# A norm between two layers, and the order in which weight tiles are streamed behind it

## The reference

```python
def attn(x):            # 16 query heads in 4 groups, head size 128, causal
    q, kg, vg = x @ Wq + bq, x @ Wk + bk, x @ Wv + bv
    return softmax(mask(q @ k.T / sqrt(128))) @ v
def ternary_quant(w):   # one scale for the whole matrix
    s = mean(abs(w))
    return clip(round(w / s), -1, 1) * s
def ffn(x):             # hidden size 5461
    h1, h3 = x @ ternary_quant(w1).T, x @ ternary_quant(w3).T
    return (silu(h1) * h3) @ ternary_quant(w2).T
x = layernorm(x + attn(x))
x = layernorm(x + ffn(x))
```

## Time and profile before

| what | before |
|---|---|
| median of 3 runs (lowest, highest) | 1499.0 us (1335.76, 1522.67) |
| the profiled execution's own time | 1341.49 us |
| its span (slowest core; all cores) | 1339.9 us (1333.4 to 1339.9) |
| PE busy, share of the span | 1272.4 us, 95% |
| DVE, ACT, POOL busy | 832.1, 458.5, 80.9 us |
| DMA, mean over the span | 321.52 MB, 240 GB/s |

### The profile page before, as it was taken

One profiled execution on the slowest core, in us unless ns is written; L12 is line 12 of the kernel. 1 busy time (PEld: TensorE's weight loads), 2 busy tenths in 40 slices (PEclk: granted clock), 3 DMA queues, 4 the chain that ended last, 5 costly groups with the idle time before them and its releaser, 6 DMA issues.

```text
span 1339.9 us, 18596 instructions; the slowest of 8 cores (1333.4 to 1339.9 us)
## 1 busy us (share of the span) xinstructions
PE 1272.4 (95%) x6824; PEld 616.3 (46%) x6824; DVE 832.1 (62%) x1200; ACT 458.5 (34%) x562; POOL 80.9 (6%) x150
## 2 busy tenths in 40 slices
PE   4999999999979889899999999999999999999996
PEld 1344556666655334344444444444444444444443
DVE  0222467777784436577766676766794388585864
ACT  0031478877887553633123232230100400000005
POOL 4000000000010000101000000000000010000000
PEclk9999999999999999899999999999999999999999
DMA  9999999999789998899867777675452964435326
GB/s 151 174 246 280 314 276 266 281 277 269 242 265 338 322 336 266 280 330 342 282 244 251 274 256 286 244 248 215 146 201 69 308 244 149 157 135 172 126 87 253
DMA packets 47761, 321.52 MB, mean 240 GB/s; under 512 B 5296, under 2 KB 5552, under 8 KB 11824
## 3 DMA queue, kind: packets, MB, share of 16 engines
q1 hardware_dynamic: 26640, 188.12, 42.2%
q0 software_dynamic: 21024, 132.13, 33.5%
HBM read 324.42 MB, written 16.78 MB: 255 GB/s over the span
## 4 chain that ended last, share of the span: by engine, by line
PE 84%; DMA 9%; DVE 3%; issue 2%; ACT 1%; POOL 1%; DVEq 0%; ACTq 0%; SPq 0%; POOLq 0%
PE ps L905 40%; PE ps L1102 22%; PE ps L413 7%; DMA ST<-w_sb 5%; PE ps L473 4%; PE ps L514 4%; DMA X<-xT 4%; PE ps L369 3%; PE ps L353 3%; PE ps L683 1%; DVE QNX L588 0%; DVE XR L536 0%; ACT PT L487 0%; DVE ACC L319 0%; ACT XB L666 0%
## 5 line engine op out<-in xcount | busy, mean ns | idle before, releaser
L905 PE MATMUL ps<-XT,QNL 128*128 128x512 bf16 x2048 | 442.4, 379 | 0.0
L905 PEld LDWEIGHTS ps<-XT,QNL 128*128 128x128 bf16 x2048 | 200.4, 98 | 241.4
L1102 PE MATMUL ps<-W2Q,G 128*128 128x512 bf16 x1376 | 297.5, 379 | 0.9 <-DVE G L928 0.6
L1102 PEld LDWEIGHTS ps<-W2Q,G 128*128 128x128 bf16 x1376 | 134.5, 98 | 163.7 <-issue 1.8
L487 ACT ACTIVATE PT<-ps 128x768 bf16<-128x768 f32 (+3 forms) x176 | 148.6, 867 | 79.1 <-PE ps L473 75.0
L588 DVE SCALAR_TENSOR_TENSOR QNL<-ST,SM,QNL 128x1024 bf16<-128x1024 f32 x128 | 164.4, 1285 | 13.7 <-DVE QNL L586 0.5
L918 ACT ACTIVATE SIL<-ps,SM 128x512 f32<-128x512 f32 x52 | 35.7, 687 | 297.0 <-PE ps L905 284.3
L316 ACT ACTIVATE ST<-ST 128x1024 f32<-128x1024 f32 (+1 forms) x79 | 108.1, 1369 | 69.7 <-DMA ST<-w_sb 69.5
L413 PE MATMUL ps<-X,WQ 128*128 128x512 bf16 x512 | 130.2, 379 | 0.8 <-DVE RCA L533 0.8
L588 DVE SCALAR_TENSOR_TENSOR W2Q<-W2F,SM,W2Q 128x1024 bf16<-128x1024 f32 x88 | 110.9, 1260 | 9.2
L905 PE MATMUL ps<-XT,QNE 128*128 128x512 bf16 x416 | 95.9, 391 | 13.0 <-DVE QNE L588 10.5
(11 more groups left out here) (73 smaller groups left out, 878.6 us busy)
## 6 DMA issues: line engine op xcount, KB each, us to landing
ST<-w_sb SPq DMA_DIRECT2D x167, 1024.0 KB, 11.0
W2F<-w_sb POOLq DMA_DIRECT2D x80, 1024.0 KB, 7.4
X<-xT POOLq DMA_DIRECT2D x16, 512.0 KB, 51.3
WQ<-wq_sb POOLq DMA_DIRECT2D x16, 512.0 KB, 12.1
XR<-xq POOLq DMA_DIRECT2D x8, 1024.0 KB, 35.8
x1spill<-XR POOLq DMA_DIRECT2D x8, 1024.0 KB, 24.8
out<-X SPq DMA_DIRECT2D x7, 1024.0 KB, 4.1
W2F<-w_sb POOLq DMA_DIRECT2D x8, 768.0 KB, 6.3
```

The source lines that it names most:

```text
L905: t = put("pe", lambda e, ec=ec: e.matmul(bank(b), qn(k)[:, ec * 128:(ec + 1) * 128], XT[:, ec * 1024 + hf * 512:ec * 1024 + (hf + 1) * 51 ...
L1102: return put("pe", lambda e: e.matmul(bank(t), G[hc][:, t * 128:(t + 1) * 128], W2Q[j % 5][:, hl * 512:(hl + 1) * 512], start=(hc == 0), s ...
```

## The change

Five edits:

- `LATE` is written anew. The number of "a" tiles behind each "w" tile, for k = 3 to 16, goes from 4 2 2 2 2 2 2 2 1 1 0 0 0 5 to 3 1 2 1 2 1 2 1 2 1 2 1 1 5; both add up to 25.
- At the last head, slots 4 and 5 are no longer spilled by `o_evac` in the norm. Their two DMAs are issued by POOL after the last kept tile has landed, and w2's loads wait for them.
- The sums of the 5 kept tiles are taken on VectorE (`tensor_reduce`, which writes no tile), instead of on ScalarE with a copy written to `W2F`.
- `o_evac(15, 5)` goes behind `ln_scale(0)` and the first two `ln_bf` of VectorE.
- The half of an absolute sum that VectorE still has to do when attention ends (`dve_bg`) goes behind `ln_stats((4, 5, 6, 7))`.

```diff
--- before.py
+++ after.py
@@ -259,7 +259,7 @@
         NWT = len(WT)
         PRE = 8
         EARLY = [3, 2, 6]
-        LATE = [4, 2, 2, 2, 2, 2, 2, 2, 1, 1, 0, 0, 0, 5]
+        LATE = [3, 1, 2, 1, 2, 1, 2, 1, 2, 1, 2, 1, 1, 5]
         spq = [("a", j) for j in range(PRE + 42)]
         ja = PRE + 42
         for k in range(NF):
@@ -306,13 +306,7 @@
                 a = col(ACC, which * 96 + ab_col[which])
                 ab_col[which] += 1
                 b = ST[s][:, k * n:(k + 1) * n]
-                if eng == "act" and j >= NAB - KEEP:
-
-                    junk = W2F[j % 3]
-                    toks.append(put("act", lambda e, a=a, b=b, junk=junk: e.activation(
-                        junk[:], b, AF.Abs, accum_out=a), [t_ab[j]] + w2_free[j % 3]))
-                    w2_free[j % 3] = [toks[-1]]
-                elif eng == "act":
+                if eng == "act":
                     toks.append(put("act", lambda e, a=a, b=b: e.activation(b, b, AF.Abs, accum_out=a),
                                     [t_ab[j]]))
                 else:
@@ -523,6 +517,7 @@
                 q_free[h + 3] = [t]
 
         t_res, t_spl = [None] * 8, [None] * 8
+        SPL_LATE = (4, 5)
         t_bn = {}
 
         def o_evac(h, ob):
@@ -540,7 +535,7 @@
             t_orel[ob] = [t]
             bfree[ob] = [t]
             if h == HH - 1:
-                for s in ss:
+                for s in [s for s in ss if s not in SPL_LATE]:
                     t_spl[s] = dma("pool", d_sp[s], XR[s][:], "spl%d" % s, [t])
 
         def bnst(s, c):
@@ -857,11 +852,6 @@
                 elif u == 10:
                     ln_stats((3,))
             if gi == NST - 1:
-                while dve_bg:
-                    try:
-                        next(dve_bg[0])
-                    except StopIteration:
-                        dve_bg.pop(0)
                 for b in range(4):
                     bfree[b] = [t_ex[NST - 2 + b // 2]]
 
@@ -869,14 +859,13 @@
 
         put("act", lambda e: e.activation(col(SM, 120), col(CFT, C_EPS), AF.Sqrt), [t_cf])
         n_att = ab_next[0]
-        if not general:
-            o_evac(HH - 1, 5)
         t = ln_scale(0)
         t_nm[0:4] = [t] * 4
         for s in range(2):
             ln_bf("dve", s)
             ln_bf("act", s + 2)
         if not general:
+            o_evac(HH - 1, 5)
             o_evac(HH - 1, 6)
         t_o15 = t_res[7]
         for s in range(4):
@@ -886,6 +875,9 @@
         for _ in range(2):
             drain(abs_go("act", 1))
         ln_stats((4, 5, 6, 7))
+
+        for gen in dve_bg:
+            drain(gen)
         t = ln_scale(4)
         t_nm[4:8] = [t] * 4
 
@@ -932,9 +924,6 @@
             t_g[(hc, hf)] = t
 
 
-        w2_free = [[x for s in range(3, 8) for x in (t_spl[s], t_xb[s])] for _ in range(3)]
-
-
         unit("w1", 0, 0)
         unit("w1", 1, 0)
         ln_bf("act", 4)
@@ -971,7 +960,7 @@
             if k > 3:
                 drain(quant(k))
                 for n in range(LATE[k - 3] if k < NF - 1 else NAB - ab_next[0]):
-                    drain(abs_go("act", 1))
+                    drain(abs_go("act" if ab_next[0] < NAB - KEEP else "dve", 1))
                     silus(max(0, 4 - n))
             for hf in range(2):
                 unit("w1", k, hf)
@@ -979,6 +968,11 @@
             silus(5)
         silus(0)
         assert ab_next[0] == NAB
+        for s in range(8):
+            if t_spl[s] is None:
+                t_spl[s] = dma("pool", d_sp[s], XR[s][:], "spl%d" % s, [t_res[s], t_ab[NAB - 1]])
+
+        w2_free = [[x for s in range(3, 8) for x in (t_spl[s], t_xb[s])] for _ in range(3)]
         b = un[0] % 8
         un[0] += 1
         scale_fin(1, scale_mm(1, scale_sum(1), b), b)
```

## The result

| | before | after |
|---|---|---|
| undisturbed runs without a profile | 1334.47, 1335.76 us | 1324.10 to 1324.82 us |
| the profiled execution (slowest span) | 1341.49 us (1339.9) | 1324.41 us (1322.9) |
| DVE, ACT, POOL busy | 832.1, 458.5, 80.9 us | 844.5, 448.9, 78.3 us |

The change makes the kernel faster by a ratio of 0.9924 (95% interval 0.9904 to 0.9943), some 10 to 11 us. The ratio, and the ratios of all experiments, leave out runs in which one die was disturbed. By the 2% that the prediction spoke of this is no change; by its own interval it is clear. The two profiled executions lie 17.0 us apart, so about 6 us of their difference are not the change's. The experiments had to find out where these lie.

The account below looks back on a forecast made before the run. The prediction took the stretch before w3 to be bound by transfers, ending with the last kept tile's landing; -10.2 us for landing and +0.3 for its sum gave -9.9, from 1341.5 to 1331.6, stated as 1331 us, range 1320 to 1341.

Parts of the forecast that it names:

- The sum: Start of w3: last kept tile's landing 10.2 us earlier, its VectorE sum 0.3 us longer, so -9.9 us, passed on whole.
- Norm, 1.5 us: Norm after attention: with o_evac and half sum moved behind, reciprocal, transposes and w1's first unit come 1.5 us earlier.
- Half sum and its slot, nothing: Norm: the half sum fits behind the statistics, and its ring slot freed at 407.6 instead of 395.7 us costs nothing.
- Late spills, 5.5 us with the norm: Load behind quant(3): two spills fewer queued and 1.5 us from the norm land it at 428.7 instead of 434.2 us.
- Order, 33 loads in 106.6 us: Stretch to the last kept tile: without the gap at 520 us, 33 loads take 106.6 instead of 111.3 us.
- TensorE stalls 1.3 us at w14: In w1, w14's half quant is there at 508.4 us against TensorE's need at 507.1: a stall of 1.3 us.
- Sum on VectorE, +0.3 us: Kept tiles' sums: slower on VectorE than ScalarE, but only the last is on the path, costing 0.3 us.
- The longer wait before w3, nothing: Before w3 TensorE idles 11 us instead of 5; slower matmuls afterwards add nothing, at worst 1.7 us.
- w2's loads later by 10 us, hidden: Behind w3's start: w2's loads come 10 us later relative to TensorE, using 10 of ScalarE's 30.3 us slack, no stall.
- the steady rate: Rival, chance 0.17: loads in the stretch come 3.47 us apart instead of 3.23, gain only 2.0 us, time 1339.5 us.
- the ring: Rival, chance 0.12: too few loads in flight in the stretch; at 3.65 us a load, time 1345.5 us.
- The faster one: Rival, chance 0.10: with the spills gone, loads take 3.0 us each, w3 starts at 534.1 and time is 1324 us.

Follow-up runs that it names:

- the pair taken on one chip: The kernel before and the changed kernel, both run again without any edit: ratios 0.9996 and 0.9933, attention to w3 153.3 and 143.9 us.
- the repeat on another chip: The kernel before, run and profiled again unchanged: ratio 0.9996, attention to w3 153.3 us.
- the order alone: The kernel before with only the new LATE, all eight spills in the norm and kept sums on ScalarE: ratio 0.9963.

## Why the prediction was right and wrong

**The mechanism and the drop were right, the level was not.** The step that failed is the last of the sum, the time from which the drop was taken. The sum said -9.9 us; the undisturbed runs without a profile fell from 1334.47 and 1335.76 to 1324.27 in the median, by 10.2 to 11.5 us, and the distance from attention to w3 by 9.4 us (153.3 to 143.9) in the pair taken on one chip. But the step "The profiled execution took 1341.5 us (span 1339.9), so 1331.6, and I say 1331" took this drop from a time that was 5.7 to 7.0 us above these runs. Against 1334.47 and 1335.76 the number 1331 is a drop of only 3.5 to 4.8 us. The text ahead of the prediction calls the profiled execution "like the third" run, but the 0.4% between them is half of the whole change. The sentence behind that step had the right row, 1335.76, and used it for the range only; 1335.76 - 9.9 = 1325.9 would have been 1.6 us off. Where these 5.7 to 7.0 us came from is seen in the table: in that profile attention ended at 392.7 us (388.2 in that of the changed kernel), and attention to w3 took 156.1 us where the repeat on another chip took 153.3. Both are the same code at another execution. Most of the second piece lies in the loads: the row of 3.23 us each, on which the sum rests, is of that execution too. From the first load over the next 25 (median of the cores) a load took 3.22 us there, 3.12 us in the same kernel's repeat, 3.16 with the order alone and 3.12 to 3.18 in the changed kernel. In the repeat, on core 0, quant(4) and quant(13) are 77.64 / 25 = 3.11 us a load apart:

```profile
437.65 0.75 DVE L586 TENSOR_SCALAR QNX<-ST,SM 128x1024 bf16<-128x1024 f32 x1 [10.60 <-DMA ST<-w_sb]
...
515.29 0.75 DVE L586 TENSOR_SCALAR QNX<-ST,SM 128x1024 bf16<-128x1024 f32 x1 [1.47 <-DMA ST<-w_sb]
```

Busy time by window, of before's profile and then of after's, shows a part of the first piece: TensorE lost 2 us at the start of attention, at nearly the same DMA share.

```profile
180.00:220.00 40.00, 37.95 (x325) 23.72 (x324) 26.87 (x64) 30.72 (x44) 1.06 (x2) 1.00 0.95 259
```

```profile
180.00:220.00 40.00, 40.00 (x341) 25.00 (x340) 28.79 (x67) 32.80 (x47) 1.06 (x2) 1.00 0.97 271
```

Why that execution was slower in both places stays open; the granted clock was 1.00 in that window. In all profiles the end of attention lay between 387 and 400 us with the kernel before, and between 387 and 402 us with the changed one.

**Point by point.**

- *Norm, 1.5 us.* The first transpose follows attention by 3.3 instead of 4.7 us, so the norm itself was right. That it reaches w3 is less sure: alone it brought 0.2 us there, on top of the two other edits 1.6 us. What the prediction did not say is that the first depends on the second.
- *Half sum and its slot, nothing.* Right.
- *Late spills, 5.5 us with the norm.* From 39.0 to 34.0 us: 5.0. The landing in 6.8 us was 6.5 on the core shown.
- *Order, 33 loads in 106.6 us.* They took 103.5 to 104.2, at 3.14 to 3.16 instead of 3.23 us each. That is not the change's doing, as the rate of the repeat shows: before took 108.4 us there and 110.5 in the first profile. The edit was worth 4.9 us in the run of it alone, against 4.7 forecast. The drop came out right because it is the width of the hole, and both ends of the difference were too long by about 3 us.
- *TensorE stalls 1.3 us at w14.* It did not wait at all: the loads came at 3.14 us, and w14 so some 2 us earlier (24 x 0.09, an estimate). The granted clock stayed at 1.00.
- *Sum on VectorE, +0.3 us.* From the last landing to w3 6.2 instead of 6.1 us. One reduction of 128x2048 took 2.29 us, not the 2.34 of two halves. As the rows had said, it is slower than ScalarE's 1.91 and 0.19 us, and it does not matter. The Trainium skill's sentence ("VectorE: DVE Perf Modes", "Rules for kernel authors"), which the prediction cites, compares VectorE's operations with each other, and there the rows do not bear it out: on 128x1024, SCALAR_TENSOR_TENSOR took 1.28 us and the reduction 1.16.
- *The longer wait before w3, nothing.* From w3 to the end the kernels with 10 us of wait took 787.9 to 788.8 us, and those with 3 to 5 us took 787.0 to 788.0: 0.7 us between the means (788.3 and 787.6) of ranges that touch, so at most a small cost, inside the bad end of 1.7.
- *w2's loads later by 10 us, hidden.* They go out at 537.5, 3 us after w3's start instead of 5.5 before it. No silu waited for them: between the 18th sum and the silu behind it 17.5 us of ScalarE's 30.3 are left, and behind w3's start TensorE waits 1.2 us in all, as before.

Of the rivals, the steady rate was kept and the ring did not run short. The faster one (1324 us) matches the time by accident: loads at 3.14 us are four tenths of the way from 3.23 to its 3.0, and the rest is the level. In its sum "427.7 + 100" the terms are each 1 us off; 428.7 + 33 x 3.0 gives the same 527.7.

## What to carry to other kernels

Take the drop from the profile, but subtract it from the time of the undisturbed runs without a profile: one profiled execution lay half a per cent off here, by attention, which the change does not touch, and by the rate of its loads. That is over half of the change itself. Compare distances between two marks over all cores, and repeat the unchanged kernel. Where a stretch ends with the last of a fixed number of loads, look for moments at which the queue is empty and for bytes that can wait, and only then at the order of the engines' work; the edit that started the next load 1.5 us earlier was worth 0.2 us while older transfers filled the queue. As soon as the landing is no longer last, the next bound takes over: here TensorE, some 7 us away in the changed kernel.

## What the runs showed of the hardware

- The same kernel took 1333.7, 1340.7 and 1346.0 us in the median on three chips. On the third, one die ran attention at a granted clock of 0.92 to 0.96 (windows of 40 us) against 1.00, and ended it some 10 us later than the other, with all four kernels run there.
- With the stream's queue full, behind the six or eight spills, loads of 1 MB came 3.1 to 3.2 us apart, at 324 to 341 GB/s (share 0.99 to 1.00, windows of 90 us) in the changed kernel and in the runs that keep its order and its number of loads. Into a queue near empty one took 6.5 to 6.8 us; behind eight spills one took 10.1 to 10.7 us.
- On VectorE, SCALAR_TENSOR_TENSOR on 128x1024 (1.28 us) was slower than TENSOR_REDUCE of as much (1.16 us).
